# One program for the opening of a fused decoder kernel, and values as three fp32r terms

## The reference

```
h = _layernorm(x, ln1_g, ln1_b)
x = _attention(h, h, sa_wq, sa_wk, sa_wv, sa_wo, sa_bo) + x
# _attention:
q = (xq @ wq).reshape(B, S, N_HEADS, D_HEAD)
k = (xkv @ wk).reshape(B, T, N_HEADS, D_HEAD)
v = (xkv @ wv).reshape(B, T, N_HEADS, D_HEAD)
attn = softmax(einsum('bihd,bjhd->bhij', q, k) * scale)
out = einsum('bhij,bjhd->bihd', attn, v).reshape(B, S, D_ATTN)
```

## Time and profile before

| | |
|---|---|
| median of 3 runs | 1820.11 us (1815.75, 1820.11, 2371.29) |
| the profiled execution's own time | 1816.95 us |
| its span, first to last instruction | 1815.2 us |
| first statistics / first projection of the front / first scores | 12.14 / 40.57 / 75.05 us |
| iterations (0,0), (0,1), (1,0) begin | 75.04, 153.77, 195.24 us |
| granted TensorE clock, mean | 0.977 |

### The profile page before, as it was taken

The page is one execution under the profiler, slowest core; times in us unless marked ns, Lnnn a source line. Parts: engine busy times, 40 slices in busy tenths (PEclk is TensorE's granted clock), DMA queues, the critical chain, the costliest instruction groups (busy, mean ns, idle before and its releaser), DMA issues. The chain is left out here.

```text
span 1815.2 us, 28598 instructions
## 1 busy us (share of the span) xinstructions
PE 1657.3 (91%) x9572; PEld 1025.1 (56%) x9572; DVE 1149.9 (63%) x2009; ACT 1067.1 (59%) x1407; POOL 959.6 (53%) x734
## 2 busy tenths in 40 slices
PE   5889999999999999988999889997898988898799
PEld 3334444444444444376666778885444436565579
DVE  4456777776777777385777753346778754776513
ACT  3436888888888888844554533311576763444452
POOL 1236888888888888951222630201334443466405
PEclk9999999999999999999999999997899999999899
DMA  2001211101110111030000010102333321000101
GB/s 91 18 24 36 68 41 48 41 35 41 38 61 35 41 35 36 24 105 27 1 1 1 13 33 24 30 13 49 91 72 96 81 63 42 9 1 1 35 16 47
DMA packets 54161, 70.82 MB, mean 39 GB/s; under 512 B 18160, under 2 KB 41868, under 8 KB 54063
## 3 DMA queue, kind: packets, MB, share of 16 engines
q1 hardware_dynamic: 54063, 69.54, 13.7%
HBM read 41.72 MB, written 2.37 MB: 24 GB/s over the span
## 5 line engine op out<-in xcount | busy, mean ns | idle before, releaser
L1412 POOL TENSOR_TENSOR x<-x,sa_p_buf 128x1024 f32<-128x1024 f32 x190 | 452.2, 2380 | 109.6 <-ACT sa_p_buf L1233 97.2
L1325 DVE TENSOR_REDUCE sa_mx<-sa_front 128x1 f32<-128x512 f32 x512 | 327.5, 681 | 109.1 <-PE sa_front L1126 107.7
L1233 ACT ACTIVATE sa_p_buf<-sa_score 128x1024 f32<-128x1024 f32 x256 | 249.2, 1024 | 115.9 <-PE sa_score L1164 115.9
L1179 PE MATMUL sa_out<-sa_p_buf,sa_v_buf 128*64 128x512 f32 x1024 | 246.2, 602 | 0.0
L607 ACT ACTIVATE sa_p_buf<-sa_score 128x1024 f32<-128x1024 f32 (+1 forms) x160 | 140.6, 943 | 75.0 <-PE sa_score L555 74.9
L402 DVE TENSOR_REDUCE sa_mx<-sa_front 128x1 f32<-128x512 f32 (+1 forms) x224 | 136.5, 651 | 31.4 <-PE sa_front L316 28.0
L2005 POOL TENSOR_TENSOR x<-x,bias_out 128x1024 f32<-128x1024 f32 x24 | 59.6, 2496 | 166.3 <-POOLq L2335 143.3
L1872 POOL TENSOR_TENSOR ca_probs<-ca_s_sb,ca_inv 128x616 f32<-128x616 f32 x64 | 77.9, 1218 | 120.8 <-DVE ca_inv L1787 120.8
L1179 PEld LDWEIGHTS sa_out<-sa_p_buf,sa_v_buf 128*64 128x64 f32 x1024 | 64.9, 136 | 126.9 <-issue 99.1
L1126 PE MATMUL sa_front<-sa_k_hi,sa_q_hi 64*128 64x512 f32 x512 | 116.7, 452 | 19.1 <-DVE sa_mx L1325 15.6
L1243 ACT ACTIVATE sa_score<-sa_m_all 128x1024 f32<-128x1024 f32 x128 | 130.8, 1033 | 1.0 <-DMA sa_m_all<-sa_m_line 0.6
(11 more groups left out here) (241 smaller groups left out, 3482.1 us busy)
## 6 DMA issues: line engine op xcount, KB each, us to landing
sa_v_buf<-o SPq DMA_DIRECT2D x16, 512.0 KB, 5.1
sa_m_all<-sa_m_line SPq DMA_DIRECT2D x16, 512.0 KB, 3.7
x<-sa_m_line SPq DMA_DIRECT2D x16, 512.0 KB, 4.4
x<-in_x SPq DMA_DIRECT2D x8, 512.0 KB, 6.7
sa_q_stack<-sa_hi SPq DMA_DIRECT2D x32, 128.0 KB, 2.6
sa_k_stack<-sa_hi SPq DMA_DIRECT2D x32, 128.0 KB, 2.6
sa_recip<-sa_den_out SPq DMA_DIRECT2D x32, 128.0 KB, 2.7
ff_w<-in_L_xattn_ff_w SPq DMA_DIRECT2D x16, 128.0 KB, 2.2
```

What stands on the lines that cost most here:

```text
L1179: mm = pe.matmul(out_ps[64 * j:64 * j + 64, :], v_buf[:, b, kt, 64 * j:64 * j + 64], p_buf[:, s % NPB, j, :], start=(kt == 0), stop=(kt == ...
L1233: nc.scalar.activation(p_buf[:, s % NPB], score_ps[s % len(score_ps)][:], ACT.Exp, scale=SCALE).then_inc(exp_done, G)
L1325: dve.tensor_reduce(mx[:, b, j, qt, half:half + 1], front_ps[bank(item, j)][:], AX.X, ALU.max).then_inc(drained, 1)
L1412: nc.gpsimd.tensor_tensor(acc[:, h], prev, cur, ALU.add).then_inc(added, 1)
```

## The change

`FirstWeights`, `constants` and the norm block ln01 are gone. `Opening` takes their place, and its parts stand in the programs of `wide_attention`, in one block and in an order written out by hand for each engine:

- SyncE loads the first four tiles of x first, then the norm's gains, tiles 4 to 7, the weights of q and k, tiles 8 to 15, the value weights, and last the context and masks.
- The norm goes in eight groups of two tiles. The groups 0 to 3 come before k0, the other four between the front items. The transposes use two PSUM banks that the attention needs later (a score bank and the output bank). The context is turned in the middle of the front, the masks are scaled in unit 2 of iteration (0,0).
- A value item is now three terms: high rows by high weights, high by low, low by high, six fp32r matmuls of 128x128 by 512. This asks for the high and low parts of the value weights, made in two halves of 512 columns: half 0 in the front (ScalarE, then GpSimd), half 1 at the start of iteration (0,1) (ScalarE, then VectorE).
- Of the 32 value items 6 stand in the front, 10 in iteration (0,0) (2, 2, 2, 2, 1, 1, 0, 0 in its units), 8 in (0,1) and 8 in (1,0), one in each unit.
- Four iterations are written out ahead of the loop in place of two, and the loads of the next stage's weights go from iteration (0,1) to (1,0). The first values are loaded into `v_buf` in two halves.

The core of the diff:

```
-    AHEAD, IN_FRONT = 8, 10
+    IN_FRONT = 6
...
+    def loads(self, sp):
...
+        rows(0)
+        for i in range(2):
+            sp.dma_start(self.lns[:, i, :], self.ln[i].rearrange("(k p) -> p k", p=P)).then_inc(self.ln_in, DMA)
+        rows(1)
+        sp.dma_start(self.wqk[:, 0], self.w["q"][:, :, at]).then_inc(self.wqk_in, DMA)
+        sp.dma_start(self.wqk[:, 1], self.w["k"][:, :, at]).then_inc(self.wqk_in, DMA)
+        rows(2)
+        rows(3)
+        sp.dma_start(self.wv, self.w["v"]).then_inc(self.wv_in, DMA)
...
     def values(self, pe, n, ps):
         half, tile = divmod(n, TT)
-        for k in range(KD):
-            mm = pe.matmul(ps, self.hT[:, k, tile * P:(tile + 1) * P], self.wv[:, k, half * HALF:(half + 1) * HALF],
-                           start=(k == 0), stop=(k == KD - 1))
+        if tile == 0:
+            pe.wait_ge(self.v_split, half + 1)
+        if half == 0:
+            self.rows_are_split(pe, tile * P // HALF)
+        parts = [(hs[:, k, at], ws[:, k, :]) for k in range(KD)
+                 for hs, ws in ((self.h_hi, self.v_hi), (self.h_hi, self.v_lo), (self.h_lo, self.v_hi))]
...
-    for u, count in enumerate((1, 1, 2, 2, 2, 2, 2, 2)):
+    for table, base, counts in ((lanes_first, lanes_first, (2, 2, 2, 2, 1, 1, 0, 0)), (lanes_second, lanes, [1] * UNITS),
+                                (lanes_third, lanes, [1] * UNITS)):
...
+                        if u == 0 and isinstance(g, int) and (g, b) == (0, 1):
+                            act.wait_ge(front_full, filled_count(0, 0, ("v", TT - 1)))
+                            first_w.split_values(act, 1)
```

More of the change, by code:

```diff
@@ L755, in tokens, with normed_rows, statistics @@
     def tokens(self, c):
         return slice(c * HALF, (c + 1) * HALF)
+    def normed_rows(self, g):
+        return self.hn[:, g % 4]
+    def statistics(self, dve, g):
+        u, step = g % 2, self.step
+        if g % 2 == 0:
+            dve.wait_ge(self.x_in[g // 2], DMA)
+        for t in range(2):
+            ins = dve.bn_stats(self.stats[:, u, t, :], self.x[:, 2 * g + t, :])
+        step(ins)
+        step.wait(dve)
+        for t in range(2):
+            ins = dve.bn_aggr(self.mv[:, u, t, :], self.stats[:, u, t, :])
+        step(ins)
+        step.wait(dve)
+        dve.tensor_scalar(self.ve[:, u], self.mv[:, u, :, 1], EPS, None, ALU.add).then_inc(self.var_done, 1)
@@ new lines, in root, with normalise @@
+    def root(self, act, g):
+        act.wait_ge(self.var_done, g + 1)
+        self.nc.scalar.activation(self.sd[:, g % 2], self.ve[:, g % 2], ACT.Sqrt).then_inc(self.sd_done, 1)
+    def normalise(self, dve, g):
+        u, step = g % 2, self.step
+        dve.wait_ge(self.sd_done, g + 1)
+        step(dve.reciprocal(self.rs[:, u], self.sd[:, u]))
+        step.wait(dve)
+        if g >= 4:
+            dve.wait_ge(self.turn_full, g - 3)
+        for t in range(2):
+            ins = dve.tensor_scalar(self.normed_rows(g)[:, t, :], self.x[:, 2 * g + t, :], self.mv[:, u, t, 0:1],
+                                    self.rs[:, u, t:t + 1], ALU.subtract, ALU.mult)
+        ins.then_inc(self.normed, 1)
@@ new lines, in evacuate @@
+    def evacuate(self, act, g):
+        if g == 0:
+            act.wait_ge(self.ln_in, 2 * DMA)
+        act.wait_ge(self.turn_full, g + 1)
+        for k in range(KD):
+            ins = self.nc.scalar.activation(self.hT[:, k, 2 * g * P:2 * (g + 1) * P],
+                                            self.turned(g)[:, k * 2 * P:(k + 1) * 2 * P], ACT.Identity,
+                                            scale=self.lns[:, 0, k:k + 1], bias=self.lns[:, 1, k:k + 1])
+        ins.then_inc(self.h_done, 1)
@@ new lines, in values, with values_bank, early_values @@
+        for m, (hs, ws) in enumerate(parts):
+            mm = pe.matmul(ps, hs, ws, start=(m == 0), stop=(m == len(parts) - 1))
+        return mm
+    def values_bank(self, n):
+        return self.turned_ps[0] if n == self.IN_FRONT - 1 else self.v_ps[n % self.NVBANK]
+    def early_values(self, pe, n):
+        if n == self.IN_FRONT - 1:
+            pe.wait_ge(self.ctx_taken, 1)
+        elif n >= self.NVBANK:
+            pe.wait_ge(self.v_made, n - self.NVBANK + 1)
+        self.values(pe, n, self.values_bank(n)).then_inc(self.v_full, 1)
@@ L974, in walk @@
         front()
-        both(0, 0)
-        both(0, 1)
-        with eng.Fori(1, NG - 1, 1) as g:
+        for g in range(STEADY):
+            both(g, 0)
+            both(g, 1)
+        with eng.Fori(STEADY, NG - 1, 1) as g:
             both(g, 0)
@@ L1150, in front_item @@
                     elif item[0] == "v":
-                        values(item[1])
+                        first_w.values(pe, item[1], front_ps[bank(item)][:]).then_inc(front_full, 1)
                     elif item[0] == "t":
@@ L1311, in front_item @@
                     kind = item[0]
-                    if kind == "v" and item[1] in IN_FRONT:
-                        return
                     fr = front_ps[bank(item)]
```

461 lines of the change are left out of this document (294 added, 167 removed).

## The result

Timed against the kernel before on one chip, the changed kernel took 1808.91 us in the median (five runs, 1805.41 to 1816.58), the kernel before 1820.2 (five runs, 1815.75 to 2371.29). The ratio is 0.9949, 95% interval 0.9933 to 0.9965: a gain of 0.5%, clear of no change, but under the 2% from which a kernel is called faster here. The run of 2371.29 us is a slow one and stands outside the ratio. The profiled execution took 1805.41 us for a span of 1803.7, against 1816.95 and 1815.2 before, so 11.5 us less. The forecast was 1804.5.

The account below looks back on a forecast made before the run. TensorE was taken to bound the iterations, with the date of the first scores deciding ahead of them. Terms -28.5, -10.7 and +26.8 gave -12.4 us, from 1816.95 to 1804.5; forecast 1799 to 1809 (0.52), wider range 1793 to 1814.

Parts of the forecast that it names:

- The opening: Everything before the first scores: norm and front overlap with 6 value items, first scores at 46.5 for 75.05, 28.5 us earlier.
- The list by hand: VectorE's queue before the first scores, dated item by item: 31.9 us of work, first statistics at 5.5, scores at 46.5.
- a sign of failure: Before the first scores: the forecast would be wrong if VectorE waited more than 7 us.
- Iteration (0,0): 14 old value items leave (-25.5), ten new come (+15.5), half clock goes (-1.7), ScalarE work (+1.0): -10.7 us.
- With another mix I expect it gone: In (0,0): a 3.4 us half-clock stretch of TensorE, costing 1.7 us, was expected to vanish.
- I charge 1: In (0,0): evacuate 7 and last high rows (2.07 us) on ScalarE ahead of the first exponents, charged 1 us.
- Iterations (0,1) and (1,0): Sixteen value items at 1.55 us on a TensorE without slack, 24.8, plus 2 for the value-weight split: +26.8 us.
- (a): Rival, chance 0.15: TensorE stays at 1.2 GHz before the first scores, costing 8 us, so 1812.5.
- (b): Rival, chance 0.15: earlier first chunk, no charge for splits or exponents, items in (0,0)'s idle time; 9.5 us more, 1795.
- (c): Rival, chance 0.06 at full or half price: TensorE waits for VectorE's copies of 26 items, 43.4 us, 1848.
- (d): Rival, chance 0.12: some 20 hand-overs among the norms in the front take 0.5 us more each, 10 us, 1814.5.
- The rule against the change: GpSimd subtractions before the first scores could slow VectorE normalisations through a shared port, up to 5.6 us, 1810; none expected.

Follow-up runs that it names:

- combined: Changed kernel with second value-weight split moved into (0,0), late value items paired, evacuate 7 and last high rows behind k's high copy: 1803.87 us, ratio 0.991 to kernel before.
- exps_first: Changed kernel with evacuate 7 and the last high rows behind unit 0's two exponents on ScalarE: unit 0 of (0,0) 9.46 us against 9.57.
- cheap_late: Changed kernel with only the first of six matmuls in each of the 16 value items of (0,1) and (1,0): (1,0) 4.9 us shorter.
- f32_values: Changed kernel with value items as the old float32 matmuls, without the value-weight splits: 1820.55 us, ratio 1.0015 to the kernel before.
- key_copy_first: Changed kernel with evacuate 7 and last high rows at the end of unit 0 of (0,0), behind k's high copy: (0,0) 3.24 us shorter.
- cheap_front: Changed kernel with only the first of six matmuls in each of the opening's six value items: first scores at 46.06 us, 0.6 later.

## Why the prediction came out as it did

**The opening** (-28.5 forecast, -29.6 measured). The list by hand held, shifted by its first term: the first statistics at 4.27 and not 5.5, ScalarE's copy of k0 at 17.48 for 18.7, t0's end at 38.91 for 40.2, the first scores at 45.47 for 46.5. In between the shift was smaller (low rows at 13.78 for 14.4), because VectorE waited for the second chunk (8.28) longer than listed. The low part of the rows on VectorE, bounded between 0.69 and 2.35 and taken at 1.2, took 1.23. What is off is the landing of a chunk of 512 KB that is alone on the queue: 3.4 us after its issue at 0.83, less than the 3.9 of the earlier trace rows, which I had taken for the floor. Apart from that first load VectorE waits 7.5 us in the opening, a little over the 7 that I named as a sign of failure; 1.6 of them lie behind its last normalisation, where the scores wait for the maxima's way through DRAM.

**Iteration (0,0)** (-10.7 forecast, -8.3 measured). Two terms are off. "With another mix I expect it gone", of the half clock, failed: there are two stretches and not none. By unit they cost 1.1 (unit 1, 12.55 against 11.42 in combined; in the second profile of the changed kernel 12.74, so 1.3) and 1.55 (unit 4, 11.17 against 9.62 in exps_first). Without them (0,0) would be 68.1 us, and the forecast said about 68. Whether a stretch falls in is partly chance: cheap_late has one, f32_values none. The other is "I charge 1" for evacuate 7 and the high rows. It was 2.1 (key_copy_first), and by another path than I gave: not the exponents but k's high copy and the bank behind it. That the total at full clock is right none the less leaves about 1 us that no run accounts for; that the ten items cost less than 15.5, in idle time that (0,0) had, would fit but is not shown.

**Iterations (0,1) and (1,0)** (+26.8 forecast, +28.3 measured). The item was put at 1.55, from a projection's 1.48 and a gap; it measured 1.66, because single items in units 1, 3, 5 and 6 wait for a bank or a copy. That is 16 x 0.11 = 1.7 us. The split was put at 2 and measured 1.7 in (0,1).

**The end** (0 forecast, -1.9 measured). That was luck: the two profiles of the changed kernel differ by more. The forecast of 1804.5 lies 0.9 us from the profiled time and 4.4 from the first median, and 8.4 from the second. The prediction saw that before's median lies 3 us above its profiled time and forecast from the profiled one; by the median it would have said 1807.5. The dates say what the sum was worth, -12.4 against -9.6.

**The rivals.** (a) a slow TensorE in the opening: it came, for a short time. By the distances of the matmuls TensorE ran at half pace up to 16.56, at a price of 0.6 us in k0, where the forecast had full clock after the first turns. Of its price of 8 us the runs show some 3: k0 and q0 at half pace cost 1.9 (combined against key_copy_first), k1 1.3 (cheap_front). For the three value items no run shows it; that VectorE waits for TensorE behind them (0.50 and 0.31 us) says that it isn't nothing. (b) more hidden: partly, the first chunk at 4.27 and items in idle time; it was given back by the clock and the key copy. (c) the copies become the wait: right in kind, at (1.66 - 1.39) = 0.27 us an item, under the 0.48 from which it would have decided. (d) the hand-overs 0.5 longer each: no, the distances between landmarks are the listed ones.

**The rule against the change.** One small operation was caught: VectorE's addition on two numbers a partition takes 1.74 us beside GpSimd's subtraction (19.78, in the rows after), 0.17 elsewhere, and the low value weights take 1.62 beside GpSimd's sums where the same shape took 1.23 alone. The Trainium skill, page "SBUF — State Buffer", section "Who interferes with whom", says that such a shared port is held for a whole instruction. The trace agrees with it: the addition ends at 21.52, as GpSimd's subtraction does (19.10 + 2.40 = 21.50). The normalisations were spared, as the list had it. The price was 0.3: q0's high part was ready at 21.14, its low part began at 21.43. In combined the same addition took 1.71, and q0's low part behind it waited 0.96 for ScalarE in any case, so it cost nothing there.

## What to carry to other kernels

Work that moves into iterations bound by one engine should stand in groups where a buffer is free, not be spread evenly: two items in one unit cost 1.39 us each (1.57 in one of four units), single ones up to 2.71 for the bank and the copy. When an engine in order gets extra work at a seam, follow each of its next results to the buffer that it frees; the 2 us on ScalarE came out on TensorE through a copy on VectorE two steps on. When a run that takes work away changes no date, look at the landmarks between before saying that the engine doesn't matter: in cheap_front a loss of 1.3 us and a gain of as much stood one behind the other. And compare such changes by dates of the same instruction in both traces: the whole time of one program moved by 7 us with the clock of stages that nobody had touched.

## What the runs showed of the hardware

The granted clock of the later stages differs between runs of one program at the same place (1.00 and 0.50 at 993 us), which is worth 6.8 us here. A half clock costs what hangs on TensorE: 3.4 us of it in a full iteration cost 1.1 to 1.55, k1 in the opening of cheap_front 1.3, q1 behind the last maxima nothing. At its start the program runs at half pace though the clock column reads 1.00: the matmuls of k0 stand 0.43 us apart and later ones 0.23, and the profiles differ in when it ends (between the third matmul of k0 and the end of q0), which moved the first scores by up to 1.9 us. An addition of two elements a partition on VectorE can take ten times as long beside a large subtraction on GpSimd (1.74 for 0.17).
